# Issuing half of the next scores ahead of the fold, and eight places for octets instead of six

## The reference

```python
def proj(x, W, bias):                       # heads H=16, dk=16, M=4 parts
    y = (x @ W.T + bias).reshape(b, s, H, dk, M)
    return jnp.transpose(y, (0, 2, 1, 3, 4))
qh, kh, vh = interfere(proj(q, Wq, bq)), interfere(proj(k, Wk, bk)), interfere(proj(v, Wv, bv))
scores = jnp.einsum('bhqdm,bhkdm->bhqkm', qh, kh) / math.sqrt(dk)
weights = jax.nn.softmax(scores, axis=3)
out = jnp.einsum('bhqkm,bhkdm->bhqdm', weights, vh)
x = x + jnp.tanh(g_xattn[0]) * (out.reshape(b, s, dm) @ Wo.T + bo)
x = x + jnp.tanh(g_ffn[0]) * ffn(layernorm(x))   # x @ W_org.T + coefficient-weighted low-rank delta
```

## Time and profile before

| | |
|---|---|
| runs | 1441.14 us median of 3 (1437.48 to 1442.63) |
| profiled execution | 1445.2 us, its span 1443.1 us |
| PE busy | 1381.8 us, 96% |
| DVE, ACT, POOL busy | 682.6, 396.1, 383.5 us |
| DMA | 224.99 MB, mean 156 GB/s |
| partial maxima, L1090 | 256 of 693 ns |
| exponentials, L1048 | 256 of 595 ns |
| waits for q_rows transfers by the first pass's matmuls (as L950's view lists them) | 19.8, 18.2 and 14.0 us |

### The profile page before, as it was taken

One profiled execution on the slowest core, in us unless ns is written; L12 is line 12 of the kernel. 1 busy time (PEld: TensorE's weight loads), 2 busy tenths in 40 slices (PEclk: granted clock), 3 DMA queues, 4 the chain that ended last, 5 costly groups with the idle time before them and its releaser, 6 DMA issues.

```text
span 1443.1 us, 22175 instructions
## 1 busy us (share of the span) xinstructions
PE 1381.8 (96%) x8464; PEld 1133.0 (79%) x8464; DVE 682.6 (47%) x1370; ACT 396.1 (27%) x728; POOL 383.5 (27%) x582
## 2 busy tenths in 40 slices
PE   7999999999999999779999999999989999999998
PEld 6888888888788888558777778788767878878787
DVE  5323132121855454456666767677776334243110
ACT  3310111111222222235455455455442120121100
POOL 1079980000500000124555555555500000000000
PEclk9999999999999999769999999999999999999999
DMA  5784655637567878866777767666542212202101
GB/s 197 205 227 161 133 151 136 154 137 148 160 173 184 189 162 238 235 187 198 212 209 219 225 198 226 204 205 200 185 164 88 88 44 88 73 30 75 42 30 58
DMA packets 181864, 224.99 MB, mean 156 GB/s; under 512 B 24064, under 2 KB 122496, under 8 KB 181760
## 3 DMA queue, kind: packets, MB, share of 16 engines
q1 hardware_dynamic: 165376, 187.62, 45.7%
q10 hardware_dynamic: 16384, 35.97, 7.9%
HBM read 137.02 MB, written 85.46 MB: 154 GB/s over the span
## 4 chain that ended last, share of the span: by engine, by line
PE 78%; DMA 12%; DVE 3%; SPq 3%; issue 2%; ACT 1%; POOL 1%; POOLq 0%; ACTq 0%; DVEq 0%
PE bank L160 19%; PE bank L162 19%; PE bank L161 19%; PE bank L985 4%; DMA q_in<-q_rows 4%; DMA early_q<-q_rows 4%; PE bank L950 3%; PE bank L970 3%; DMA first_q<-q_rows 2%; PE bank L300 2%; PE bank L933 2%; PE bank L935 2%; PE bank L934 2%; PE bank L334 2%; SPq L194 1%
## 5 line engine op out<-in xcount | busy, mean ns | idle before, releaser
L1090 DVE TRANSPOSE_TENSOR_REDUCE part<-bank 128x16 f32<-128x512 f32 x256 | 167.8, 693 | 32.7 <-PE bank L950 30.7
L1048 ACT ACTIVATE probT<-bank 128x512 f32<-128x512 f32 x256 | 138.6, 595 | 120.7 <-PE bank L970 120.5
L520 DVE SCALAR_TENSOR_TENSOR stage_lo<-bank,bias_mixed,stage_hi 128x512 fp32r<-128x512 f32 x64 | 47.9, 749 | 227.8 <-ACT stage_hi L522 227.6
L160 PE MATMUL bank<-place_a,w_hi 128*128 128x512 f32 x384 | 151.0, 393 | 1.8 <-DVE place_a L153 1.8
L162 PE MATMUL bank<-place_a,w_lo 128*128 128x512 f32 x384 | 149.6, 390 | 0.0
L161 PE MATMUL bank<-place_a,w_hi 128*128 128x512 f32 x384 | 149.4, 389 | 0.0
L522 ACT ACTIVATE stage_hi<-bank,bias_mixed 128x512 fp32r<-128x512 f32 x64 | 44.0, 688 | 272.3 <-PE bank L162 255.9
L933 PE MATMUL bank<-place_a,oT_hi 128*128 128x512 f32 x256 | 108.4, 423 | 0.7 <-ACT gated L1012 0.7
L1433 DVE SCALAR_TENSOR_TENSOR raw_d<-bank,gates,raw_d 128x512 f32<-128x512 f32 x32 | 24.0, 751 | 173.3 <-PE bank L162 173.3
L160 PE MATMUL bank<-place_a,yT_hi 128*128 128x512 f32 x256 | 102.4, 400 | 0.0
L162 PE MATMUL bank<-place_a,yT_lo 128*128 128x512 f32 x256 | 101.1, 395 | 0.0
(11 more groups left out here) (209 smaller groups left out, 2790.0 us busy)
## 6 DMA issues: line engine op xcount, KB each, us to landing
k_rows<-stage_hi SPq DMA_DIRECT2D x128, 128.0 KB, 2.5
v_pad<-v_out SPq DMA_DIRECT2D x32, 512.0 KB, 2.6
v_place<-v_pad ACTq DMA_DIRECT2D x32, 512.0 KB, 4.7
q_rows<-stage_hi SPq DMA_DIRECT2D x124, 128.0 KB, 2.5
early_q<-q_rows SPq DMA_DIRECT2D x122, 100.0 KB
q_in<-q_rows SPq DMA_DIRECT2D x84, 100.0 KB
k_in<-k_rows SPq DMA_DIRECT2D x42, 196.0 KB
k_rows<-stage_lo SPq DMA_DIRECT2D x64, 128.0 KB, 2.5
```

The source lines that it names most:

```text
L160: nc.tensor.matmul(bank_ap, sh, mh, start=(i == 0), stop=False)
L520: lambda bank: nc.vector.scalar_tensor_tensor(out=lo[:], in0=bank[:], scalar=bias, in1=hi[:].bitcast(F32), op0=ALU.add, op1=ALU.subtract),
L1048: act.activation(probT[o % NPT][:, i].rearrange("k a p q -> k (a p q)"), two_bank[i][:], ACT.Exp).then_inc(s_exp, 1)
L1090: dve.tensor_reduce(part[o % NS][:, :, 2 * i:2 * i + 2, :].rearrange("k a p b -> k a (p b)"), one_bank[i][:].rearrange("k (a b t) -> k a b ...
```

## The change

The places go from six to eight, and the loads from three slots ahead to five. Octets 4 to 7 now wait for POOL's clearing, which has four tiles instead of two. On PE the first half of the next octet's first pass is issued ahead of the fold; it waits for the partial maximum that frees its bank and no longer for the reduce, which the second half now waits for. The fold and the reduce behind it use the second bank. DVE waits once, before the loop, for the end of the projection's evacuations.

```diff
-        KQ, EARLY = 6, 4
+        KQ, EARLY, AHEAD = 8, 4, 5
...
                 def load_oct(o):
                     if o < KQ:
-                        sp.wait_ge(s_zero[o % 2], 1)
+                        sp.wait_ge(s_zero[o % 2], (o - EARLY) // 2 + 1)
                         sp.wait_ge(s_stage[o % 2], 96 * ((NG * KC + o) // 2 + 1))
                     else:
                         sp.wait_ge(s_two, 2 * (o - KQ) + 2)
...
                     if i < 2:
-                        sp.wait_ge(s_two, 2 * (OCTS - KQ + i) + 2)
+                        last = max(o for o in range(OCTS) if o % KQ == 2 + i)
+                        sp.wait_ge(s_two, 2 * last + 2)
...
                     if 1 <= s <= OCTS:
                         place_max(s - 1)
-                    if s == KQ - LAG:
+                    if s == 0:
+                        for o in range(EARLY, AHEAD):
+                            load_oct(o)
+                    if s + AHEAD == KQ:
                         projected(sp)
-                    if EARLY <= s + LAG < OCTS:
-                        load_oct(s + LAG)
-                    if s == KQ - LAG:
+                    if s + AHEAD < OCTS:
+                        load_oct(s + AHEAD)
+                    if s + AHEAD == KQ:
                         sp.dma_start(bo_row[:], bo.partition_broadcast(P)).then_inc(s_bo, 16)
-                    if s == OCTS - KQ + 4 + LAG:
+                    if s == OCTS - 2 + LAG:
...
                             pe.wait_ge(s_kq[slot], 48 * (o // KQ + 1))
                             if o:
-                                pe.wait_ge(s_max, o)
+                                pe.wait_ge(s_part, 2 * o - 1)
+                        elif o:
+                            pe.wait_ge(s_max, o)
...
                         pe.wait_ge(s_part, 2 * o + 2)
-                        pe.transpose(one_bank[0][0:32, 0:P], part[o % NS][:].rearrange("k a p b -> k (a p b)"),
+                        pe.transpose(one_bank[1][0:32, 0:P], part[o % NS][:].rearrange("k a p b -> k (a p b)"),
...
                     work, h = proj_at(s), half_at(s, 0)
-                    first_pass(s, 0)
+                    if s == 0:
+                        first_pass(s, 0)
                     first_pass(s, 1)
                     if h is not None:
                         values(h)
+                        first_pass(s + 1, 0)
                         fold(s)
                     for part_of in work[:(len(work) + 1) // 2]:
                         project(*part_of)
                     second_pass(s - LAG)
                     if h is None:
+                        first_pass(s + 1, 0)
                         fold(s)
...
+                dve.wait_ge(project_line.emptied, len(project_line.jobs))
                 for s in range(SLOTS):
...
-                        dve.tensor_reduce(negmax[at][:], one_bank[0][0:32, 0:P].rearrange("c (i q) -> c q i", i=4), AX.X,
+                        dve.tensor_reduce(negmax[at][:], one_bank[1][0:32, 0:P].rearrange("c (i q) -> c q i", i=4), AX.X,
```

## The result

| | before | changed |
|---|---|---|
| median of 18 runs each | 1439.7 us (1436.4 to 1444.0) | 1434.9 us (1432.3 to 1439.0) |
| ratio | | 0.9968, 95% interval 0.9957 to 0.9979 |
| profiled execution | 1445.2 us | 1435.5 us, span 1433.4 |

The change makes the kernel faster by 0.32%. So the direction came out, and the size did not: 4.8 us by these medians. From profile to profile the time fell by 9.7 us.

A forecast was written before the change was run, and what follows sets the result against it. TensorE was taken to set the time, with DMA waits in the attention stage. Terms -18.5, +3.2, +6.7, 0 and -4.0 sum to -12.6: 1445.2 becomes 1432.6, less 4.1 for the median gives 1428.5 us; range 1416 to 1442.

The forecast's parts named there:

- first-pass waits: From 651 to 1015 us, loads two slots earlier remove all stalls of first passes for their octet's rows: -18.5 us.
- The chain fold, reduce, raw_o, values: In the slot before the values, a fold 0.24 us later delays the values equally: +6.7 us over 28 slots.
- The closed loop of the first slots: Slots 1 to 5: loop falls from 3.03 us to 2.38, or about 2.5 with other work; gain 2.8 us.
- the steady terms: Terms for the attention stage after 651 us: -18.5 first-pass waits, +3.2 placing waits, +6.7 later fold.
- the last one of the sum: Converting the profiled execution's forecast, 1432.6 us, to a median of runs by taking off 4.1 us: 1428.5.
- The placing waits: After 651 us, second passes wait for placed maxima lagging 0.8 us: +3.2 us, bounds 0 and +15.8.
- The order's cost: Putting half a first pass ahead of the fold delays the values 0.24 us per value slot: +6.7 us.
- the fold's wait after the values: In the slot after the values, the fold's 28 waits of 0.20 us stay: 0, bounds -4 and +1.
- The start: First sixteen slots, 589 to 651 us: shorter loop and earlier loads, partly lost to placing waits; -4.0 us together.
- Rival 1: After 651 us, placing lag is 1.74 us and 15.8 us of stall come back: 1443 us; chance 0.22.
- rival 3: The queue no longer drains between value slots, costing 0.3 to 0.6 us a cycle above rival 1: 1453; chance 0.08.
- rival 2: Everything hides: lag below 0.5 us and values' wait not fixed by the fold; about 1419 us, chance 0.22.

The follow-up runs named there:

- h2: Changed kernel, but in the slot before the values both halves of the next first pass are issued behind the fold again; median 1429.7 us.
- e4: Changed kernel with DVE's reciprocals and raw_o issued ahead of its wait for the fold in the slot before the values; median 1428.2 us.
- e2: Changed kernel with only the new TensorE order kept: six places and loads three ahead, as before the change; median 1483.7 us.
- e1: Changed kernel with only the new loads kept (eight places, five ahead) and the TensorE order of before; median 1427.9 us.
- e3: Changed kernel with loads four slots ahead and not five, eight places kept; median 1425.1 us.
- f2: Kernel before, with its old TensorE order, but eight places and loads four ahead; median 1420.5 us.
- f3: Changed kernel with raw_o issued ahead of the wait for the fold and loads four ahead; median 1417.8 us.
- f4: Kernel before, with its old TensorE order, but eight places, loads four ahead and raw_o issued ahead of the wait for the fold; median 1419.7 us.
- h3: Changed kernel with the placing of the maxima issued by GpSimd on its own queue and not by SP; median 1556.4 us.
- h1: The changed kernel, unchanged, run and profiled a second time; median 1435.2 us.

## Why the prediction was wrong

**What was right.** All first-pass waits went (predicted -18.5 us for 111 slots). The chain fold, reduce, raw_o, values was named, with its place and about its size: idle 0.54 and not 0.30, back to 0.30 in h2 and gone in e4. The closed loop of the first slots fell to 2.37 us, computed as 2.38, until the second passes come in (weight loads of the second half pass, and one second pass):

```profile
595.46 0.50 PEld L956 LDWEIGHTS bank<-early_q,second_k 98*128 98x128 f32 x2 [0.67 <-DVE negmax L1112]
...
597.83 0.50 PEld L956 LDWEIGHTS bank<-early_q,early_k 98*128 98x128 f32 x2 [0.67 <-DVE negmax L1112]
...
600.21 0.50 PEld L956 LDWEIGHTS bank<-early_q,early_k 98*128 98x128 f32 x2 [0.66 <-DVE negmax L1112]
...
605.50 0.93 PEld L976 LDWEIGHTS bank<-early_q,second_k 98*128 98x128 f32 x4 [2.13 <-issue]
```

And the sum of the steady terms, -18.5 + 3.2 + 6.7 = -8.6, is near what two profiles of each kernel show: 353.3 and 354.4 before, 346.6 and 344.1 after, -8.5 on the mean.

**The step that failed** is the last one of the sum: "The median of the runs is 4.1 us under that execution". It took the 4.1 us as a constant of the measurement, and so carried a loss of the profiled execution over to ordinary runs. For the changed kernel the difference was 0.6 us. Of the 7.8 us by which the gain fell short (12.6 forecast, 4.8 measured), 4.9 are this step (9.7 us between the first profiles, 4.8 between medians) and 2.9 the terms below: 1.9 in the steady part and 1.3 in the start, less 0.3 elsewhere. Between profiles the change is worth -10.4 us on the mean of both pairs (1445.4 to 1435.0), between medians -4.8. Two of two profiled executions of the kernel before lie 4.6 and 5.5 us above its median, and e2's, which waits for loads as well, 3.3; both of the changed kernel and those of e1, e3, e4, f2 and f3, without first-pass waits from 651 us on, lie within 1 us of theirs. So in these runs a change that removes those waits gains 3 to 6 us less between medians than between profiles. Why is open. The rest does not sort itself by waits for transfers: h2 and f4, with 13.3 and 9.0 us of placing waits, lie 3.2 and 1.3 us above their medians, but e4 with 16.1 us only 0.6 above, and h3 lies 6.4 us below. No run measured a transfer with and without the profiler. What is shown is that two profiles of the kernel before agree with each other and not with its ordinary runs.

**Two terms were mis-sized and nearly cancelled.** The placing waits came to 7.2 us of the steady part (346.6 less 27 x 12.57), in the second profile 4.7, where I had 3.2 for a lag of 0.8 us. The lag itself was a choice between two bounds, so that 3.2 came this near is partly luck. (The place of the cycle that it was worked out from has 28 distances and not 27; their sum is right.) e3 shows that the place in the queue is their cause in the changed kernel: issued ahead of the load and not right behind it, the placings cost nothing there. (The lead went from five to four with it; no run parts the two.) It is not the whole of it: with shorter cycles (f2, f3, f4) there are 2.7, 4.7 and 9.0 us with four ahead, too. The order's cost was 0.15 us a cycle and not 0.24 (12.57 against 12.42), and the fold's wait after the values, put at 0, did go: 28 waits of 0.20 us before, none after. The two fit: f3 against f4 shows a gain of 0.09 from it, and 0.24 less 0.09 is 0.15.

**The start** was put at -4.0 us and brought 2.7 between the first profiles and 1.2 between the means (72.0 to 70.8). In both profiles first-pass waits of about 9 us ahead of the fourth half's values (8.8 and 9.3 in the two profiles of the kernel before) went, and waits of the second pass for placings grew from 3.0 and 2.0 us to 5.6 and 9.1. The prediction had said that the one would turn into the other, and took too little off for it. The longest of h1:

```profile
612.27 0.93 PEld L976 LDWEIGHTS bank<-early_q,early_k 98*128 98x128 f32 x4 [3.67 <-DMA early_q<-neg]
```

The row of 605.50 above shows one thing more, in the first profile alone: slot 4's second pass stood for 2.1 us. By the program it waits for the exponentials, and ACT did not start them before the last stores of the queries had landed:

```profile
603.50 1.28 ACT L1057 ACT_TABLE_LOAD   x1 [10.99 <-DMA q_rows<-stage_hi]
```

In the kernel before and in h1, ACT had been waiting for PE there:

```profile
602.72 1.28 ACT L1048 ACT_TABLE_LOAD   x1 [10.64 <-PE bank L970]
...
601.20 1.28 ACT L1057 ACT_TABLE_LOAD   x1 [10.22 <-PE bank L976]
```

In h1 the second pass of that slot stood for 0.17 us, and its start was no shorter (71.3 us), so the stores are not what limits the start as a rule. Three early loads are issued before 599 us now, where there was one, and they may delay the stores. No run tested that link alone. e1 has the same early loads and the old order, and its start (69.9) is no longer than the changed kernel's, so with five ahead the new order brought nothing there that shows. With four ahead the starts are 65.4 to 67.3 us whatever the order; e3 against f2 has 1.9 us for the new order, f3 against f4 0.3, one profile each.

**Rivals.** Rival 1 (the placing takes the whole stall over, 15.8 us) and rival 3 did not happen, since 4.7 to 7.2 us came back; neither did rival 2, since the values do wait longer. The rule of the Trainium skill that the prediction cited (page DMA: Bandwidth & Descriptors, section "Why a DMA increments its semaphore by 16 and not by 1"), by which an octet's transfers would lie on 14 and 10 engines, has no bearing that a run shows: cycles went down to 12.11 us at a mean DMA share of 0.74 (f3, 651 to 1015 us), above the 11.4 us worked out from it.

## What to carry to other kernels

A stall that the trace shows for a transfer belongs to that execution: set the profiled time against several unprofiled ones before a gain is promised, and do not count on the difference to stay once the stall is gone. Take a change with two edits apart: here the longer lead alone gave 14 us, and the order beside it cost about 7 us with the lead and 41 without it, where it asked for each load a microsecond sooner. After a large transfer gets more lead, look at the small one queued behind it, whose user got none; putting it ahead of the load (four steps ahead and not five) gave 7 us more in the steady part and, with the start, about 10 in all.

## What the runs showed of the hardware

A small transfer issued from GpSimd was far dearer than expected: in h3 GpSimd stood idle for 185 us in 70 waits ahead of the issues, where the profile shows nothing that it waited for, and a placing took 3.3 us in the median from issue to landing, 7.3 at most.

A stall of 2.1 us until 774.4 us in the changed kernel was followed by a stretch with a granted clock of 0.66 (windows: stretch, length, busy us of PE, PEld, DVE, ACT, POOL, clock, DMA share, GB/s):

```profile
770.00:775.00 5.00, 3.35 (x20) 2.60 (x19) 2.09 (x4) 2.66 (x5) 1.75 (x3) 1.00 0.76 214
775.00:780.00 5.00, 5.00 (x75) 4.16 (x74) 2.43 (x6) 1.71 (x4) 2.95 (x4) 0.66 0.33 102
```

The values in it took 2.46 us of weight loads and not 1.72, so a single late placing cost 2.1 us and then at least 0.7 more. Not every stall of this length did so: no stretch of 5 us below 1.00 followed the wait of 2.48 us before 698.28 in the kernel before, nor one of 2.10 us before 703.44 in f2.
